# A layer's first tiles turned earlier, its first heads sent in chunks, and eight tiles turned inside the attention loop

## The reference

```python
h = layer_norm(emb_word[input_ids] + emb_pos[:S][None], emb_ln_s, emb_ln_b)
for l in range(4):
    q, k, v = heads(h @ Wq[l] + bq[l]), heads(h @ Wk[l] + bk[l]), heads(h @ Wv[l] + bv[l])
    a = band_attention(q, k, v, mask)
    h = layer_norm(h + merge(a) @ Wo[l] + bo[l], ln1_s[l], ln1_b[l])
    f = gelu(h @ W1[l] + b1[l])                      # 192 -> 768
    h = layer_norm(h + f @ W2[l] + b2[l], ln2_s[l], ln2_b[l])
```

## Time and profile before

| | |
|---|---|
| median of 3 runs (lowest, highest) | 2112.12 us (2109.9, 2117.12) |
| the profiled execution: its time, its span | 2105.01 us, 2103.2 us |
| PE, PEld, DVE, ACT, POOL busy | 75%, 63%, 65%, 53%, 34% of the span |
| mean granted TensorE clock | 0.876 |
| chain that ended last, by engine | PE 48%, DVE 24%, issue 12%, ACT 6%, DMA 4%, POOL 3% |
| attention loops begin (first score, L472) | 93.0 us in layer 0; the last attention's last one is at 1765.0 us |

### The profile page before, as it was taken

One profiled execution on the slowest core, in us unless ns is written; L12 is line 12 of the kernel. 1 busy time (PEld: TensorE's weight loads), 2 busy tenths in 40 slices (PEclk: granted clock), 3 DMA queues, 4 the chain that ended last, 5 costly groups with the idle time before them and its releaser, 6 DMA issues.

```text
span 2103.2 us, 47757 instructions
## 1 busy us (share of the span) xinstructions
PE 1575.0 (75%) x14634; PEld 1320.4 (63%) x14634; DVE 1356.9 (65%) x3622; ACT 1109.5 (53%) x3351; POOL 717.1 (34%) x989
## 2 busy tenths in 40 slices
PE   0588777798787798786898783875945887649993
PEld 0477666576576676675676672754944666449993
DVE  4688865688765789665888655243436998544444
ACT  0499632698523799323898221323524997225651
POOL 5644123534122542133541231012544340025551
PEclk9999889899798899798999795877976999669996
DMA  5868000875000955003864000004746580137875
GB/s 133 167 111 101 16 1 2 152 96 83 1 1 25 155 80 72 1 2 52 136 96 49 1 1 12 1 21 143 239 126 91 83 100 2 40 120 239 242 233 167
DMA packets 191388, 178.63 MB, mean 85 GB/s; under 512 B 23056, under 2 KB 176208, under 8 KB 190992
## 3 DMA queue, kind: packets, MB, share of 16 engines
q1 hardware_dynamic: 183824, 158.19, 38.4%
q0 software_dynamic: 7296, 17.18, 2.5%
HBM read 132.96 MB, written 42.34 MB: 83 GB/s over the span
## 4 chain that ended last, share of the span: by engine, by line
PE 48%; DVE 24%; issue 12%; ACT 6%; DMA 4%; POOL 3%; SPq 1%; DVEq 1%; ACTq 0%; POOLq 0%
DVE ptl L688 7%; PE bank L1261 6%; PE bank L483 5%; PE bank L562 4%; ACT pth L615 3%; PE bank L501 2%; PE bank L364 2%; DVE neg_max L682 2%; ACT prob L604 2%; PE bank L1247 2%; PE bank L382 2%; DVE h L805 2%; DMA kx<-qk_rows 1%; PE bank L472 1%; PE bank L386 1%
## 5 line engine op out<-in xcount | busy, mean ns | idle before, releaser
L604 ACT ACTIVATE prob<-bank,neg_max 128x192 f32<-128x192 f32 (+1 forms) x960 | 417.1, 440 | 67.5 <-DVE neg_max L682 32.2
L688 DVE TENSOR_TENSOR ptl<-bank,pth 128x512 f16<-128x512 f32 x480 | 329.3, 686 | 34.7 <-ACT pth L615 26.6
L682 DVE TENSOR_REDUCE neg_max<-bank 128x2 f32<-128x384 f32 (+1 forms) x480 | 273.6, 570 | 92.9 <-PE bank L472 90.3
L483 PE MATMUL bank<-ident,prob 128*128 128x128 f32 x1920 | 310.0, 285 | 0.0
L615 ACT ACTIVATE pth<-bank 128x512 f16<-128x512 f32 x480 | 286.9, 598 | 6.4 <-PE bank L483 6.4
L569 ACT ACTIVATE xx<-bank 128x256 fp32r<-128x256 f32 x256 | 94.2, 384 | 365.8 <-PE bank L364 360.0
L501 PE MATMUL bank<-v,pth 128*128 128x32 bf16 x1920 | 199.4, 180 | 107.1 <-DVE ptl L688 94.0
L501 PEld LDWEIGHTS bank<-v,pth 128*128 128x128 f16 x1920 | 154.0, 96 | 197.6 <-DVE ptl L688 187.4
L483 PEld LDWEIGHTS bank<-ident,prob 128*128 128x128 f32 x1920 | 205.6, 143 | 0.2
L604 ACT ACTIVATION_READ_ACCUMULATOR prob<-bank,neg_max 128x1 f32 x960 | 202.6, 211 | 0.0
L503 PE MATMUL bank<-v,ptl 128*128 128x32 bf16 x1920 | 193.6, 176 | 0.0
(11 more groups left out here) (273 smaller groups left out, 4250.0 us busy)
## 6 DMA issues: line engine op xcount, KB each, us to landing
xn<-in_e_seg SPq DMA_DIRECT2D x34, 768.0 KB, 6.8
qx<-qk_rows SPq DMA_DIRECT2D x240, 96.0 KB, 5.0
kx<-qk_rows SPq DMA_DIRECT2D x240, 96.0 KB, 7.2
qk_rows<-fbuf SPq DMA_DIRECT2D x80, 192.0 KB, 2.8
w<-in_e_w SPq DMA_DIRECT2D x23, 576.0 KB, 4.6
qk_rows<-piece_c SPq DMA_DIRECT2D x40, 192.0 KB, 3.0
hb<-in_e_w SPq DMA_DIRECT2D x11, 576.0 KB, 4.3
y_rows<-mask SPq DMA_DIRECT2D x8, 768.0 KB, 8.7
```

What stands on the lines that cost most here:

```text
L483: last = nc.tensor.transpose(bank[BT[p % 2]][:, (2 * e + c) * P:(2 * e + c) * P + P], prob[:, qt, hd % PROBS, c * P:c * P + P], ident[:, :])
L604: nc.scalar.activation(prob[:, qt, hd % PROBS, c0:c0 + n], scores_at(u // 2, n)[:, u % 2, :], ACT.Exp, bias=neg_max[:, tile_no % 3, hd:hd ...
L682: nc.vector.tensor_reduce(neg_max[:, t % 3, hd:hd + 2], scores_at(p, D if banded else S), AX.X, ALU.max, negate=True).then_inc(max_ready.s ...
L688: nc.vector.tensor_tensor(ptl[:, p % 2, :], bank[BT[p % 2]][:, :], pth[:, p % 3, :], ALU.subtract)\
```

## The change

It has four parts.

1. **The first four tiles** of layer it+1 are turned under the feed-forward part of layer it, ahead of its steps 20 and 21 (`under`, new argument `first`), for layer 0 ahead of the loop. DVE splits them in `dve_tail` behind the normalisation of group 2.
2. **The last group's** statistics and normalisation move to the head of the next layer: `dve_last_stats` behind `dve_pieces` of item 2, `dve_affine` behind item 6, POOL's reciprocal root ahead of `pool_v(0)` and its four sums between `pool_v(0)` and `pool_pieces(1)`. PE waits for the last residual (`y_read`) ahead of item 1.
3. **Inside the loop**: `beside` keeps tiles 4 to 7 behind items 2 and 3. Tiles 8 to 15 are turned one by one in steps 2, 3, 5, 6, 8, 9, 11 and 12 (`next_turn`), at the end of the step, in bank 3, which the projections of steps 4, 7 and 10 use too.
4. **Heads by chunks**: each of group 0's three items has its own counter, and as soon as its write has landed, four heads of the first sequence are read with 12 DMAs, so 36 for that sequence in place of 12.

Parts 3 and 4 hold for the last attention too. The core of the diff:

```diff
-        def pe_transpose(pe, it, s, t, src, ready, turn, n):
+        def pe_transpose(pe, it, s, t, src, ready, turn, n, inside=False):
             pe.wait_ge(ready.sem, ready.at(turn, n))
-            pe.wait_ge(xx_ready.sem, xx_ready.at(it, s - 1))
+            pe.wait_ge(xx_ready.sem, xx_ready.at(it, s if inside else s - 1))
+            o = bank[BM[0] if inside else BX[t % 2]]
...
-            steps = {2 + i: (lambda i=i: (tile(GT + 2 * i), tile(GT + 2 * i + 1))) for i in range((NT - GT) // 2)}
-            steps["xx"] = xx
+            steps = {2: lambda: (tile(GT), tile(GT + 1)), 3: lambda: (tile(GT + 2), tile(GT + 3))}
+            steps["xx"], steps["inside"] = xx, lambda t: tile(t, True)
...
+        def next_turn(p):
+            if 2 <= p < 2 + 12 and p % 3 != 1:
+                return 2 * GT + 2 * (p // 3) - (p % 3 == 0)
+            return None
...
+            for i in range(2):                       # under
+                steps[FC * (NG - 1) + 2 + i] = lambda i=i: (first(2 * i), first(2 * i + 1))
...
         def pe_attention(pe, it, banded, w, before):
             for n in range(ITEMS + AHEAD):
+                if n == 1:
+                    pe.wait_ge(y_read.sem, y_read.at(it, 0))
...
-            pe.wait_ge(xx_ready.sem, xx_ready.at(*before["xx"](NT)))
             for p in range(PAIRS + 5):
...
                 if next_projection(p):
                     g, i = next_projection(p)
+                    if i == 0:
+                        pe.wait_ge(xx_ready.sem, xx_ready.at(*before["xx"](NT)))
+                    elif p and next_turn(p - 1):
+                        pe.wait_ge(xx_ready.sem, xx_ready.at(*before["xx"](next_turn(p - 1) + 1)))
                     pe_qkv(pe, it, g, i, w)
+                if next_turn(p):
+                    if next_projection(p - 1):
+                        g, i = next_projection(p - 1)
+                        pe.wait_ge(vf_ready.sem, vf_ready.at(it, 4 * g + i - 3 + 1))
+                    before["inside"](next_turn(p))
...
         def act_attention(act, it, banded, split):
+                if next_turn(p):                     # end of step p
+                    split["inside"](next_turn(p))
...
         def dve_attention(dve, ch, it, banded, split):
+                if n == 2 and banded:                # behind dve_pieces of item 2
+                    dve_last_stats(dve, ch, it)
                 if n in split:
                     split[n]()
+                if n == ITEMS - 1 and banded:
+                    dve_affine(dve, ch, it, 0, NG - 1, 1)
             for p in range(PAIRS + 8):
...
+                if p and next_turn(p - 1):           # behind dve_max, dve_lo and dve_v of step p
+                    split["inside"](next_turn(p - 1))
                 if p >= 11 and (p - 11) % 6 < 3 and (p - 11) // 6 < NT:
                     dve_finish(dve, ch, it, (p - 11) // 6, (p - 11) % 6, banded)
...
+                if 1 <= g < NG:                      # dve_tail
                     dve_stats(dve, ch, it, 1, g - 1, y_read)
...
+                if 1 <= g < NG:
                     dve_affine(dve, ch, it, second(g - 1), g - 1, 1)
...
+                if g == NG - 1:
+                    for t in range(GT):
+                        dve_split(dve, it + 1, t, t)
...
+            def read(b, heads, done):                # sp_heads
                 for a, dst in enumerate((qx, kx)):
                     for r, slot in enumerate(SLOTS):
+                        src = qk_rows[g % 2][a, slot[a], DH * heads.start:DH * heads.stop, b % 2 * S:b % 2 * S + S]
+                        sp.dma_start(dst[DH * r:DH * r + DH, b % 3, heads, :], src.rearrange("(h r) n -> r h n", r=DH))\
+                            .then_inc(done.sem, 16)
+            if g == 0:
+                for i in range(4):
+                    if i < 3:
+                        sp.wait_ge(first_pieces.sem, first_pieces.at(it, i + 1))
+                        write(i, first_out[i])
+                    if i:
+                        sp.wait_ge(first_out[i - 1].sem, first_out[i - 1].at(it, 32))
+                        read(0, slice(4 * (i - 1), 4 * i), first_in[i - 1])
+                read(1, slice(0, HEADS), qk_in[1])
...
             with pool.Fori(0, L) as it:
                 ch.enter(it, 160)
+                pool_rstd(pool, ch, it, 0, NG - 1, 1e-12)
                 pool_v(pool, ch, it, 0)
+                pool_hb(pool, it, normed(2, NT - GT) - 2 * NT, NG - 1, row_bo)
                 pool_pieces(pool, ch, it, 1)
```

More of the change, by code:

```diff
@@ L754, in dve_residual, with dve_last_stats, dve_stats @@
                     .then_inc(read.sem, 1)
-        def dve_stats(dve, ch, it, half, g, read):
+        def dve_last_stats(dve, ch, it):
+            dve_stats(dve, ch, it, 1, NG - 1, y_read, NT)
+        def dve_stats(dve, ch, it, half, g, read, back=0):
             c = []
@@ L900, in sp_heads, with write @@
         def sp_heads(sp, it, g):
-            for i in range(3):
-                if g == 0:
-                    sp.wait_ge(first_pieces.sem, first_pieces.at(it, i + 1))
-                else:
-                    sp.wait_ge(next_pieces.sem, next_pieces.at(it, 3 * (g - 1) + i + 1))
+            def write(i, done):
                 for a in range(2):
                     sp.dma_start(qk_rows[g % 2][a, :, 64 * i:64 * i + 64, :].rearrange("z r n -> r z n"),
-                                 pieces[i][64 * a:64 * a + 64, :, :]).then_inc(pieces_out.sem, 16)
@@ new lines, in sp_heads @@
+            if g == 0:
[7 more added lines that the diff above has]
+                read(1, slice(0, HEADS), qk_in[1])
+            else:
+                for i in range(3):
+                    sp.wait_ge(next_pieces.sem, next_pieces.at(it, 3 * (g - 1) + i + 1))
+                    write(i, pieces_out)
+                sp.wait_ge(pieces_out.sem, pieces_out.at(it, 96 * g))
+                for b in (2 * g, 2 * g + 1):
+                    if b % 2:
+                        sp.wait_ge(s_done.sem, s_done.at(it, PAIRS // B * (b - 2)))
+                    read(b, slice(0, HEADS), qk_in[b % 3])
@@ L1522, in _ @@
             pool.wait_ge(rows_bo.sem, 16)
-            for g in range(NG + 1):
-                if g < NG:
+            for g in range(NG):
+                if g < NG - 1:
                     pool_rstd(pool, ch, 0, g + 1 - NG, g, 1e-12)
```

91 lines of the change are left out of this document (48 added, 43 removed).

## The result

The changed kernel took 2211.5 us (median of 4 runs, 2209.3 to 2216.2) against 2111.0 us (4 runs, 2104.7 to 2117.1): ratio 1.048, 95% interval 1.044 to 1.052. It is slower, as forecast, but by 100 us where 72 were forecast, and 8.5 us above the range's upper end of 2203.

A forecast was written before the change was run, and what follows sets the result against it. Bounds: DVE's normalisation after feed-forward, DMA's and POOL's chains in the head, the loop's first steps at 1.43 us each. Feed-forward +38.6, head -24.5, loop +57.8 make +71.9: forecast 2184 us, range 2140 to 2203.

The forecast's parts named there:

- Turns inside the loop: Steps 2 to 12 of each attention: PE and DVE run in turn over bank 3, +57.8 us in all.
- if the lower clock holds on: Upper bound of the loop's term: 15 us an attention, 75 us in all; the lower bound was 15 us in all.
- a sign of being wrong: Loop's first steps: a clock that stays down through them would put the time above 2190 us.
- the loop's 17.2 us: Steps 2 to 12: room between the loop's term, 57.8 us, and its upper bound, 75 us.
- the feed-forward part's 3.4: Feed-forward part, four layers: room between its term, 9.65 us a layer, and its upper bound, 10.5.
- The stall in the feed-forward part: Ahead of step 21, PE waits for DVE's splits behind group 2's normalisation: 9.65 us a layer, 38.6 us in four.
- The head: Start of layers 1 to 3: first scores of the loop come 8.2 us earlier in each, 24.5 us gained.
- Chunks, layer 0, the last attention: Reading heads by chunks, layer 0's head and the last attention's head: each was to change the time by 0.
- The turns as mere load: Loop: turns only load the engines, costing 15 us there, 2141 us in all; chance 0.07.
- an unhindered PE in the feed-forward part: Feed-forward part: DVE reaches the splits in time, 3 us in place of 38.6, 2148 us in all; chance 0.05.
- the early start of the loop: Head: the first chunk starts the loop without ACT standing at POOL's piece, 75 us less, 2108 us; chance 0.06.
- The late chunk: Step 4 of the loop: the last chunk lands 5 us late in five attentions, 25 us, 2209 us; chance 0.06.

The follow-up runs named there:

- the run with extra work: The changed kernel with eight extra matmuls in each of steps 2 to 13 and 38 in step 1 of each attention: 2185.1 us, ratio 1.041.
- the faster one with them: The changed kernel with all tiles turned in the head, tiles 12 to 15 behind items 7 and 8, early splits, late sums: 2094.2 us, ratio 0.989.
- the run with filled waits: The changed kernel with eight extra matmuls of 128 columns in each of steps 2 to 13 of an attention: 2206.3 us, ratio 1.051.

## Why the prediction was wrong

*What failed* is the term "Turns inside the loop", in its size: +57.8 us forecast, +82.1 measured. The mechanism, PE and DVE running in turn because bank 3 has one occupant, was right, and so was the sum of its pieces at the full clock (28.0 us in layer 2 and 138.9 us in all five in the run with extra work, for 27.5 and 138.0). The step that failed is the choice between the bounds: I took PE's pieces from rows at the full clock for a pattern that gives PE a new idle time in each round, and left "if the lower clock holds on" to the upper bound. It did, in four of five. The prediction had named this as a sign of being wrong, a clock that stays down through the loop's first steps and a time above 2190 us, and that is what came.

That bound itself was low, 15 us an attention, 75 in all, where 18.5 were measured in layers 1 and 3 and 82.1 in all. The upper end of the range is 19 us above the forecast, which is the whole of the loop's 17.2 us and half of the feed-forward part's 3.4, and not half of each as the prediction words it; half of each would have been 2194 us. The result is beyond 2203 by 8.5 us, about the loop's 7.1 us above its bound and the 8.0 us behind maximum 13, less the 6 us by which the profile of the kernel before lies under its median.

*The stall in the feed-forward part*: where it stands, between the last two residuals, it cost 88.3 - 49.7 = 38.6 us, as forecast, with 6.36 us of idle time for 6.8. The other 3.8 of the 42.4 us came ahead of it, from maximum 95 to group 2's residual, a stretch that takes 102.5 to 104.3 us a layer before and 103.6 to 105.7 after; by what is not shown. The run with the early splits shows that 1.6 us a layer of the 9.65 are the turns and not the stall.

*The head*: 8.7 us a layer for 8.2. Errors cancel in part: the sums take 2.2 us for 3.6, but POOL starts the values only at Y + 12.3 for 11.35, behind the reciprocal root of the last group (1.4 us, which the sum left out of POOL's chain), and takes half a microsecond longer for them. POOL's piece ends at Y + 29.2 for 29.6. Its end at POOL's piece was right: moving the sums away moved maximum 2 by 1.7 us.

*Chunks, layer 0, the last attention*: 0 forecast, -1.1 to +2.2 measured.

*Behind maximum 13* I forecast nothing and 8.0 us came. With the turns inside alone it was 4.8 us, with all tiles in the head -4.5 us, with the turns in pairs -9.2 us, so it goes with the turns one by one and not with the chunks, as far as one execution each can tell. By what wait is not shown.

*The rivals.* The turns as mere load, an unhindered PE in the feed-forward part and the early start of the loop did not come: the first maxima were there at Y + 20 and ACT did stand at POOL's piece. The late chunk did not come in the changed kernel: that its price, 2209 us, lies near the result is luck. Its reads of 32 KB landed in 1.8 and 1.9 us in the median, where those of 96 KB before took 5.0 and 7.2. The late chunk came in small in two other kernels, the one before with the chunks alone and the faster one with them: pair 4 waited 0.9 to 1.5 us in some layers. Both also waited 1.3 to 4.6 us a layer at pair 24, which no rival had.

*Still open*: what decides between the two levels. With 38 extra matmuls ahead of the loop the upper one won in three attentions of five and with 70 in none; it won in layer 2 of the changed kernel and not in layer 1, though PE's waits in the loop up to the point at which they part are alike (1.10 and 0.25 us); and in the last attention of the run with filled waits the lower one stayed for 24.8 us without any wait.

## What to carry to other kernels

Where two engines are made to hand one buffer back and forth, price the round from the rows, and then price it again with every piece of PE at the lower clock: each wait is a new idle time, and here the two differed by a fifth of these steps (34.1 us for 28.0). Before work is moved under other work, find in each engine's stream what stands ahead of it: with four splits behind a normalisation the end of a feed-forward part took 22.1 us, with the splits ahead of it 14.0, and 12.4 without them. And what is brought forward is worth only as much as the chain that ends next: here POOL's piece, then ACT's copy, then the third sequence's DMA.

## What the runs showed of the hardware

The lower clock lasted for 34.3 us (layer 1 of the changed kernel) in which PE was busy for 28.4 us, with no wait over 0.6 us from the fourth round on. The upper clock lasted through rounds with waits of 0.92 us in layer 2. The same 208 matmuls took 28.1 us at 0.94 and 34.1 at 0.50 in one execution. With the idle time filled, the clock in layer 0 was 0.50 up to 99 us, 0.81 in the next 3 us and 1.00 in the 3 after; in the last attention of the same execution it was 0.50 for 24.8 us of unbroken work.

Of POOL's four sums in the row of 3.61 us in the earlier trace rows, the first took 1.95 us and the others 0.60; in the head after, all four took 0.59, the same instruction on the same shape.
